# Expert loops written out, row sums on VectorE in layer 0, and halves and quarters of the probabilities added by GpSimd in layer 1

## The chip, the cores and the metric

The kernel runs on one core of one Trainium2 chip. The metric is the device time of one execution in microseconds (us), and lower is better. TensorE (PE in the rows; PEld is its weight load) multiplies matrices and transposes, VectorE (DVE), ScalarE (ACT) and GpSimd (POOL) do the rest, and SyncE (SP) issues most of the DMAs. Every engine works through a queue of its own in order; between engines only semaphores order the work.

## The reference

Two transformer layers on x of 16 batches x 256 tokens x 128 channels, all in float32. Each layer is a modulated layer norm, an attention with a gated residual, another modulated norm, and a mixture of experts with a gated residual. Cut to what matters:

```
# layer 0: causal attention, 16 heads of 8 channels, with relative keys and values
att = softmax(mask(q k^T / sqrt(8) + q . rk[t - s]))
y   = att v + sum_s att[t, s] rv[t - s];  out = y Wproj + bproj
# layer 1: sparse attention: per batch the k = 76 most important of 256 keys
importance = relu(x wi1^T + bi1) wi2^T + bi2;  top 76 keys kept
att = softmax(q k^T / sqrt(8)) over the kept keys;  out = (att v) wo^T + bo
# experts (both layers): 8 experts, the best 2 for each of 4096 tokens
layer 0: out = sum_k w_k * (gelu(x c_fc[e]) c_proj[e]);        128 -> 512 -> 128
layer 1: r = x + (gelu(x Wi[e]) * sigmoid(x Wg[e])) Wo[e];  layer norm of r, weighted
```

## The kernel before

The program is a row of blocks, each ended by a barrier of all engines: setup; for each layer norm, projections, attention, norm with the routers' logits, routing, experts, combine; and the output. `wait_ge(semaphore, n)` holds the engine's queue until the count is reached, and the instructions behind it wait too.

**Layer 0 attention** (`rel_attention_phase`, lines 510 to 765). A batch is worked through in four steps j = 0 to 3 of 64 queries; step j has 64(j + 1) keys. A global counter m counts the steps. In round m TensorE computes the scores of step m (L606, L614) into `ps_s`, four PSUM banks that hold one step only, so the scores of step m + 1 wait until VectorE is through with step m (`wait(pe, subbed, m)`). VectorE's `shift(m)` adds the causal mask (L704), takes the row maximum (L707) and subtracts it (L710); ScalarE takes the exponential (L741). Behind the scores TensorE transposes the probabilities of step m - 1 (`turn`, L629, copied back by ScalarE, L749), multiplies those of m - 2 with the relative values (`rel_values`, L642; `mask`, L716, on VectorE), and in certain steps the values of the batch (`values`, L656), a second product with a matrix of ones, `ones_diag`, that gives the row sums spread to the layout of the result (L660), the `fold` of the relative part (L669) and the output projection (`project`, L676). VectorE's `normalize` takes the reciprocal of the 128x256 sums (L721) and multiplies (L723). GpSimd prepares the masked queries (`diag`, L403; `rel`, L411) and `v_diag`, and adds the result to x (L581).

**Layer 1 attention** (`sparse_attention_phase`, lines 940 to 1172). A batch has two rounds of 128 queries, m = 2b and m = 2b + 1. GpSimd's `choose(b)` (L1148) builds the 0/1 matrix `select` of the kept keys; TensorE's `gather(b)` (L986, L989) multiplies it with the keys and values; VectorE's `spread(b)` (L1058) and ScalarE's `split_values(b)` (L1106) lay them out. TensorE's queue in an even round m = 2b is: `scores(m)` (L999), `gather(b + 1)`, `turn(m - 1, (0, 1))` (L1010), `project(b - 2)` (L1032), `turn(m - 1, (2, 3))`. In an odd round it is `scores(m)`, two turns with `values(b - 1)` (L1020) between and behind them, and `denominators(b - 1)` (L1027). `gather(b + 1)` waits for `selected`, which `choose(b + 1)` raises. VectorE's queue in a round is `normalize` (L1084, L1086; even rounds), `shift(m)` (maximum L1065, subtraction L1068), `row_sums(m - 1)` (L1074, over all 16 x 76 probabilities of a row), in even rounds `invert(b - 1)` (L1080) and `spread(b + 1)`. ScalarE copies the four transposed groups (L1119), with `gate` (L1125) between the second and the third in even rounds, and then takes the exponential `exp(m)` (L1112). GpSimd's queue sets the order at its end:

```
choose(0); memset v_diag; choose(1)
for b in range(B + 2):
    if b >= 1 and b + 1 < B: choose(b + 1)
    if 1 <= b <= B: widen(b - 1)      # waits for invert(b - 1)
    if b >= 2: add(b - 2)
```

`widen` (L1155) spreads the reciprocals of the row sums, and `denominators` transposes them.

**Experts** (`expert_phase`, lines 1432 to 1728). 39 tiles of 256 token slots. Per tile GpSimd issues two indirect DMAs that fetch token rows (L1696) and two that scatter the result (L1704), SP loads the expert's weights, and TensorE does the first layer (L1526), a transpose of a later tile's rows (L1536) and the second layer (L1545). The tiles 0 to 3 and 32 to 38 are written out; the 28 between run in hardware loops of 7 passes over four tiles (`tiles`, `Fori`). VectorE copies the indices of each tile into `token_now` (L1586, L1618) and `dest_now` (L1612), at a place that is the same in every pass of the loop, and the indirect DMAs read them there.

## Time and profile before

| what | us |
|---|---|
| median of 3 runs | 1541.46 (1540.43 to 1545.56) |
| the profiled execution, its device time | 1546.82 |
| its span in the profile | 1544.9 |
| layer 0 attention in it | 77 to 581 |
| layer 0 experts | 667 to 877 |
| layer 1 attention | 990 to 1164 |
| layer 1 experts | 1247 to 1506 |
| TensorE matmul, VectorE, ScalarE, GpSimd busy | 1246.8, 890.5, 650.9, 562.8 |

The profiled execution took 5.4 us more than the median, 0.35%. Busy time is that of the whole span; the stages have different limits, so each is read by itself. A matmul in float32 stands in the profile as two records, and the ends of matmuls are modelled, so the distance between the starts of two blocks tells more than their durations.

### The profile page before, as it was taken

The page shows a single profiled execution, that of the slowest core. Times are in us where ns is not written, and L with a number is a line of the kernel's source. Part 1 is how long each engine was busy: PE and PEld are TensorE (multiplying, and loading weights), DVE is VectorE, ACT ScalarE, POOL GpSimd, SP SyncE. Part 2 cuts the span into 40 slices and gives each one's busy share as a digit, 9 for nine tenths or more (in the row PEclk, how much of TensorE's full clock was granted, in tenths as well). Part 3 has the DMA queues.
Part 4 walks back from the last instruction along what each step waited for, and adds up shares of the span by engine and source line. Part 5 has one row for each costly group of instructions (what it writes and reads, how often), then busy time and mean ns, then how long its engine had stood idle before and what let it go on. Part 6 is the DMA issues. An engine that isn't in the chain of part 4 may idle for free. (4 is left out here: it accounts for less than half of the span.)

```text
span 1544.9 us, 46711 instructions
## 1 busy us (share of the span) xinstructions
PE 1246.8 (81%) x19038; PEld 1035.9 (67%) x19038; DVE 890.5 (58%) x2078; ACT 650.9 (42%) x1298; POOL 562.8 (36%) x636
## 2 busy tenths in 40 slices
PE   5778899988999887578877559688887569999973
PEld 4457677766777777567777444355556569999973
DVE  6455565645657644821111175899994737677664
ACT  3233343333434435024343262266765036666533
POOL 2231231211312200457777400112110437888760
PEclk7889999999999995579999858799997569999985
DMA  5632223122230002045455430000003045655536
GB/s 153 156 101 38 33 31 52 38 31 30 32 49 12 4 3 69 1 121 163 149 152 151 96 89 1 1 1 1 1 1 86 12 107 178 182 172 178 173 74 165
DMA packets 110896, 119.27 MB, mean 77 GB/s; under 512 B 28064, under 2 KB 78464, under 8 KB 110208
## 3 DMA queue, kind: packets, MB, share of 16 engines
q1 hardware_dynamic: 100736, 96.23, 24.5%
q0 software_dynamic: 9984, 20.47, 5.4%
q8 instruction: 139, 2.28, 0.6%
q14 instruction: 37, 0.30, 0.1%
HBM read 97.79 MB, written 21.91 MB: 77 GB/s over the span
## 5 line engine op out<-in xcount | busy, mean ns | idle before, releaser
L1572 ACT ACTIVATE act_x_m<-ps_h_x_m,fc_bias_x_m 128x256 f32<-128x256 f32 x468 | 196.2, 470 | 182.3 <-PE ps_h_x_m L1526 167.4
L1526 PE MATMUL ps_h_x_m<-x_T_x_m,fc_x_m 128*128 128x256 f32 x936 | 245.3, 413 | 3.0 <-issue 1.9
L1526 PEld LDWEIGHTS ps_h_x_m<-x_T_x_m,fc_x_m 128*128 128x128 f32 x936 | 227.7, 329 | 6.4 <-issue 4.3
L749 ACT ACTIVATE probT<-ps_t 128x512 f32<-128x512 f32 (+1 forms) x192 | 104.0, 591 | 194.1 <-PE ps_t L629 194.1
L1704 POOL DMA_INDIRECT y_dram<-y_x_m,dest_now_x_m x156 | 155.4, 996 | 63.2 <-issue 43.3
L1696 POOL DMA_INDIRECT x_rows_x_m<-h_dram,token_now_x_m x156 | 154.9, 993 | 52.8 <-issue 44.7
L1545 PE MATMUL ps_o_x_m<-proj_x_m,act_x_m 128*128 128x128 f32 x1248 | 154.2, 277 | 2.6 <-DVE act_x_m L1596 2.6
L1545 PEld LDWEIGHTS ps_o_x_m<-proj_x_m,act_x_m 128*128 128x128 f32 x1248 | 147.6, 194 | 3.0 <-DVE act_x_m L1596 2.8
L704 DVE TENSOR_TENSOR ps_s<-ps_s,future 128x512 f32<-128x512 f32 x64 | 44.7, 699 | 169.4 <-PE ps_s L614 169.4
L1612 DVE COPY dest_now_x_m<-dest_m 128x2 int32 (+1 forms) x78 | 14.4, 184 | 204.8 <-PE ps_o_x_m L1545 171.0
L741 ACT ACTIVATE prob<-prob 128x512 f32<-128x512 f32 (+1 forms) x64 | 81.2, 1269 | 100.9 <-DVE prob L710 100.9
L629 PE MATMUL ps_t<-ident,prob 128*128 128x128 f32 (+1 forms) x768 | 107.1, 283 | 8.5 <-ACT probT L749 7.8
L614 PE MATMUL ps_s<-e_rel,q_rel 64*32 64x64 f32 (+3 forms) x4096 | 98.8, 312 | 10.8 <-issue 10.5
L629 PEld LDWEIGHTS ps_t<-ident,prob 128*128 128x128 f32 (+1 forms) x768 | 80.6, 132 | 35.3 <-ACT probT L749 15.9
L707 DVE TENSOR_REDUCE neg_max<-ps_s 128x8 f32<-128x512 f32 (+1 forms) x64 | 95.4, 1491 | 2.2
L710 DVE TENSOR_TENSOR prob<-ps_s,neg_max 128x512 f32<-128x512 f32 (+1 forms) x64 | 95.4, 1491 | 2.2
L574 POOL COPY v_diag<-v 128x128 f32<-128x128 f32 x32 | 8.4, 291 | 231.9 <-PE ps_y L669 231.8
L1119 ACT ACTIVATE probT<-ps_t 76x512 f32<-76x512 f32 x128 | 69.0, 590 | 49.6 <-PE ps_t L1010 49.6
L614 PEld LDWEIGHTS ps_s<-e_rel,q_rel 64*32 64x32 f32 x4096 | 65.5, 109 | 36.0 <-issue 26.8
L656 PE MATMUL ps_y<-probT,v_diag 128*32 128x128 f32 x1536 | 82.4, 274 | 6.9 <-ACT upd L756 3.6
L1313 POOL TENSOR_SCALAR column_hit_m<-column_m,part_f_m,choice_id_m 128x78 f32<-128x78 f32 x64 | 48.4, 760 | 104.7 <-DVEq L1393 102.1
L1580 ACT ACTIVATE x_T_x_m<-ps_x_x_m 128x256 f32<-128x256 f32 x78 | 29.9, 384 | 129.2 <-PE ps_x_x_m L1536 129.2
(261 smaller groups left out, 2359.6 us busy)
## 6 DMA issues: line engine op xcount, KB each, us to landing
q_spread<-q_dram SPq DMA_DIRECT2D x256, 64.0 KB
fc_x_m<-L_ffn_c_fc SPq DMA_DIRECT2D x39, 256.0 KB
proj_x_m<-L_ffn_c_proj SPq DMA_DIRECT2D x39, 256.0 KB
fc_x_m<-L_ffn_Wi SPq DMA_DIRECT2D x39, 256.0 KB
fc_x_m<-L_ffn_Wg SPq DMA_DIRECT2D x39, 256.0 KB
proj_x_m<-L_ffn_Wo SPq DMA_DIRECT2D x39, 256.0 KB
got_c_m<-y_dram SPq DMA_DIRECT2D x32, 256.0 KB, 5.2
h_dram<-h_rows_m SPq DMA_DIRECT2D x16, 256.0 KB, 2.3
```

The source lines that it names most:

```text
L614: x = pe.matmul(ps_s[rows(i), 2 * z + hp, s * n:(s + 1) * n], a.q_rel[64 * z:64 * (z + 1), b % 2, tile, hp, :], a.e_rel[64 * z:64 * (z + 1 ...
L629: x = pe.transpose(ps_t[0:ks, t % 2, p * P:(p + 1) * P], prob[:, m % 2, p, at:at + ks], k.ident[:, :])
L656: pe.matmul(ps_y[rows(p), 0, P * half:P * (half + 1)], v_diag[:, b % 2, ch, 4 * p + h, :], view(probT[:, half + ch, p, 0, :], TB * h, [[QU ...
L707: dve.tensor_reduce(neg_max[:, m % 2, :, :], split(ps_s[:, 0, :], m), AX.X, ALU.max, negate=True).then_inc(maxed, 1)
L710: dve.tensor_tensor(split(prob[:, m % 2, 0, :], m), split(ps_s[:, 0, :], m), view(neg_max[:, m % 2, :, :], 0, [[2, GROUPS], [1, 2], [0, n] ...
L741: act.activation(p_, p_, ACT.Exp).then_inc(expd, 1)
L749: act.activation(probT[0:ks, store(m, ch), :, (2 * j + s) % 4, :], ps_t[0:ks, t % 2, :].rearrange("p (g c) -> p g c", g=GROUPS), ACT.Copy) ...
L1526: m = pe.matmul(ps_h[:, l, g, f % 2, :], fc[:, slot, l, f:FF:FK], x_T[:, slot % 2, :], start=True, stop=True)
L1545: m = pe.matmul(ps_o[:, s % 2, h * P:(h + 1) * P], act1[:, s % 2, f, h * P:(h + 1) * P], proj[:, s, f, :], start=f == 0, stop=f == FK - 1)
L1572: m = act.activation(out[:, slot % 2, f, :], ps_h[:, l, g, f % 2, :], ACT.Tanh if l else ACT.Gelu, scale=0.5 if l else 1.0, bias=fc_bias[: ...
L1696: pool.indirect_dma_start(out=x_rows[:, slot, h, :], out_offset=None, in_=k.h_dram, in_offset=bass.IndirectOffsetOnAxis(ap=token_now[:, sl ...
L1704: pool.indirect_dma_start(out=k.y_dram, out_offset=bass.IndirectOffsetOnAxis(ap=dest_now[:, slot, h:h + 1], axis=0), in_=y[:, slot, h, :], ...
```

## The change

It has three parts.

1. **Experts.** The hardware loops go; all 39 tiles are written out with constants as semaphore counts, and the indirect DMAs read their indices straight from `r.token` and `r.dest`. The copies into `token_now` and `dest_now` and their semaphore go.
2. **Layer 0 attention.** The products with `ones_diag` go. VectorE sums the rows of each step (`row_sums`), inverts the 32 sums of a row once a batch (`invert`), GpSimd lays the reciprocals on a diagonal (`spread_inv`), four matmuls bring them to the result's layout (`denominators`), and `normalize` copies and multiplies. The orders on TensorE, GpSimd and ScalarE change, and two small tables replace `ones_diag`.
3. **Layer 1 attention.** GpSimd adds the two halves of each row of 76 probabilities and then the halves of that (`fold_rows`), VectorE's `row_sums` sums the 19 that are left. `project` moves behind the second turn, `normalize` behind `shift`, its copy to ScalarE, `gate` behind the exponential.

```diff
 rel_attention_phase, GpSimd:
+            def spread_inv(b):
+                pool.wait_ge(inv_ready, b + 1)
+                wait(pool, inv_turned, b)
+                pool.tensor_tensor(inv_diag[:, :, :, :], view(row_inv[:, b % 2, 0, :], 0, [[NB, GROUPS], [1, NB], [0, BLOCK]]),
+                                   view(a.own_query[:, 0, :], 0, [[0, GROUPS], [0, NB], [1, BLOCK]]), ALU.mult).then_inc(inv_spread, 1)
-            for b in range(B + 1):
+            for b in range(B + 2):
                 if b + 1 < B:
                     wait(pool, score, NP * b)
                     diag(pool, a, b + 1)
+                if b >= 2:
+                    add(b - 2)
+                if b + 1 < B:
                     rel(pool, a, b + 1)
+                if 1 <= b <= B:
+                    spread_inv(b - 1)
+                if b + 1 < B:
                     values(b + 1)
-                if b >= 1:
-                    add(b - 1)
 TensorE:
-                        for p in range(GROUPS):
-                            pe.matmul(ps_y[rows(p), 1, P * half:P * (half + 1)], a.ones_diag[:, h, :],
-                                      view(probT[:, half + ch, p, 0, :], TB * h, [[QUADRANT, 16], [1, TB]]),
-                                      start=False, stop=False, skip_group_check=True)
+            def denominators(b):
+                pe.wait_ge(inv_spread, b + 1)
+                for p in range(GROUPS):
+                    x = pe.matmul(ps_y[rows(p), 1, :], a.head_rows[:, :, :], inv_diag[:, p, :, :],
+                                  start=False, stop=True, skip_group_check=True)
+                x.then_inc(inv_turned, 1)
...
+                if j == 0:
+                    if exists(m - 2):
+                        rel_values(m - 2)
+                    if exists(m - 1):
+                        turn(m - 1, 0)
+                        values(b - 1, 0, (2, 3))
+                        turn(m - 1, 1)
+                elif j == 1:
+                    if exists(m - 1):
+                        turn(m - 1, 0)
+                        turn(m - 1, 1)
+                    if exists(m - 2):
+                        rel_values(m - 2)
+                    if b >= 1:
+                        values(b - 1, 1, (0, 1, 2, 3))
+                elif j == 2:
+                    if exists(m - 1):
+                        turn(m - 1, 0)
+                        turn(m - 1, 1)
+                    if exists(m - 2):
+                        rel_values(m - 2)
+                    if b >= 1:
+                        denominators(b - 1)
+                        fold(b - 1)
+                else:
+                    if exists(m - 1):
+                        turn(m - 1, 0)
+                    if exists(m - 2):
+                        rel_values(m - 2)
+                    if b >= 1:
+                        project(b - 1)
+                    if exists(m - 1):
+                        turn(m - 1, 1)
+                        values(b, 0, (0, 1))
 VectorE (row_sums behind shift and mask, invert where j == 0):
+                dve.tensor_reduce(row_sum[:, b % 2, :, 2 * j:2 * j + 2], split(prob[:, m % 2, 0, :], m), AX.X, ALU.add).then_inc(summed, 1)
...
+                dve.reciprocal(row_inv[:, b % 2, :, :], row_sum[:, b % 2, :, :]).then_inc(inv_ready, 1)
...
-                dve.reciprocal(rden[:, :], ps_y[:, 1, :]).then_inc(rden_ready, 1)
+                dve.tensor_copy(inv_y[:, :], ps_y[:, 1, :]).then_inc(inv_copied, 1)

 sparse_attention_phase, TensorE:
                 if exists(m - 1):
                     turn(m - 1, (0, 1))
-                if u == 0 and b >= 2:
-                    project(b - 2)
                 if u == 1 and 1 <= b <= B:
                     values(b - 1, (0, 1))
                 if exists(m - 1):
                     turn(m - 1, (2, 3))
+                if u == 0 and b >= 2:
+                    project(b - 2)
 VectorE:
-                dve.wait_ge(expd, m + 1)
-                dve.tensor_reduce(row_sum[:, m // 2 % 2, m % 2, :], prob[:, m % 2, :, :, :].rearrange("p g h r -> p (g h) r"),
-                                  AX.X, ALU.add).then_inc(summed, 1)
+                dve.wait_ge(quartered, m + 1)
+                dve.tensor_reduce(row_sum[:, m // 2 % 2, m % 2, :], part_sum[:, m % 2, :, :], AX.X, ALU.add).then_inc(summed, 1)
...
+                if exists(m):
+                    shift(m)
                 if u == 0 and b >= 2:
                     normalize(b - 2)
-                if exists(m):
-                    shift(m)
 ScalarE:
+                if u == 0 and b >= 2:
+                    copy_inv(b - 2)
                 if exists(m - 1):
                     copy(m - 1, (0, 1))
-                if u == 0 and b >= 2:
-                    gate(b - 2)
-                if exists(m - 1):
                     copy(m - 1, (2, 3))
                 if exists(m):
                     exp(m)
+                if u == 0 and b >= 2:
+                    gate(b - 2)
 GpSimd:
+            def fold_rows(m):
+                r = prob[:, m % 2, :, :, :].rearrange("p g h r -> p (g h) r")
+                pool.wait_ge(expd, m + 1)
+                wait(pool, quartered, m)
+                pool.tensor_tensor(half_sum[:, :, :], r[:, :, 0:KEPT // 2], r[:, :, KEPT // 2:KEPT], ALU.add).then_inc(halved, 1)
+                pool.wait_ge(halved, m + 1)
+                wait(pool, summed, m - 1)
+                pool.tensor_tensor(part_sum[:, m % 2, :, :], half_sum[:, :, 0:KEPT // 4], half_sum[:, :, KEPT // 4:KEPT // 2],
+                                   ALU.add).then_inc(quartered, 1)
...
             for b in range(B + 2):
+                if 1 <= b <= B:
+                    fold_rows(2 * b - 1)
+                    widen(b - 1)
                 if b >= 1 and b + 1 < B:
                     choose(b + 1)
-                if 1 <= b <= B:
-                    widen(b - 1)
+                if b < B:
+                    fold_rows(2 * b)
                 if b >= 2:
                     add(b - 2)

 expert_phase:
-        def tiles(eng, step, first=0, last=XTILES):
-
-            for j in range(first, UNROLL):
-                step(j // UNROLL, j % UNROLL)
-            with eng.Fori(1, LOOP_END) as i:
-                for s in range(UNROLL):
-                    step(i, s)
...
-                dve.tensor_copy(token_now[:, s, :], r.token[:, bass.ds(2 * (j + UNROLL), 2)]).then_inc(token_ready, 1)
...
-                                            in_offset=bass.IndirectOffsetOnAxis(ap=token_now[:, slot, h:h + 1], axis=0)).then_inc(x_in[slot], 16)
+                                            in_offset=bass.IndirectOffsetOnAxis(ap=r.token[:, 2 * j + h:2 * j + h + 1], axis=0)).then_inc(x_in[slot], 16)
```

## Rows read from the trace of the kernel before

**Rows 1.** Windows by stage: stretch, length, busy PE PEld DVE ACT POOL, PEclk, DMA, GB/s

```profile
77.00:581.00 504.00, 439.53 (x14078) 354.53 (x14063) 294.06 (x290) 192.26 (x273) 115.76 (x79) 0.96 0.21 35
...
990.00:1164.00 174.00, 150.78 (x1468) 98.13 (x1467) 155.39 (x160) 115.08 (x193) 31.03 (x63) 0.97 0.01 1
...
1247.00:1506.00 259.00, 235.22 (x1326) 228.78 (x1326) 166.68 (x544) 143.22 (x352) 187.97 (x196) 0.95 0.54 159
```

**Rows 2.** Timeline of one batch of layer 1 attention: start, duration, engine, line

```profile
1062.52 0.79 PE L999 MATMUL ps_s<-k_diag,qT 32*128 32x304 f32 x8
...
1063.25 0.67 PE L986 MATMUL ps_g<-select,kv 128*128 128x76 f32 x4
1063.43 1.42 DVE L1065 TENSOR_REDUCE neg_max<-ps_s 128x16 f32<-128x1216 f32 x1
...
1064.88 1.43 DVE L1068 TENSOR_TENSOR prob<-ps_s,neg_max 128x1216 f32<-128x1216 f32 x1
...
1066.22 1.41 DVE L1074 TENSOR_REDUCE row_sum<-prob 128x16 f32<-128x1216 f32 x1
...
1067.66 0.35 DVE L1080 RECIPROCAL row_inv<-row_sum 128x32 f32<-128x32 f32 x1
...
1068.08 0.40 POOL L1155 COPY inv_wide<-row_inv 128x256 f32<-128x256 f32 x1 [8.34 <-DVE row_inv L1080]
...
1068.48 1.07 PE L1010 MATMUL ps_t<-ident,prob 128*76 128x128 f32 x8 [1.15 <-ACT prob L1112]
...
1069.14 0.93 POOL L1148 TENSOR_SCALAR select<-places,rank 128x76 f32<-128x76 f32 x2
...
1072.85 0.79 PE L999 MATMUL ps_s<-k_diag,qT 32*128 32x304 f32 x8
```

**Rows 3.** Timeline of the first rounds of layer 1 attention, at the lower clock

```profile
987.83 0.94 POOL L1148 TENSOR_SCALAR select<-places,rank 128x76 f32<-128x76 f32 x2 [78.56 <-SPq L941]
...
988.82 1.14 PE L986 MATMUL ps_g<-select,kv 128*128 128x76 f32 x4 [10.40 <-POOL select L1148]
...
997.20 3.24 PE L1010 MATMUL ps_t<-ident,prob 128*76 128x128 f32 x16
```

**Rows 4.** Windows around one of TensorE's gaps in layer 0 attention, columns as Rows 1

```profile
329.00:336.00 7.00, 0.23 (x4) 0.00 (x0) 0.00 (x0) 0.00 (x0) 0.00 (x0) 0.86 0.51 68
336.00:339.00 3.00, 2.98 (x35) 2.18 (x36) 1.33 (x2) 0.37 (x1) 0.00 (x0) 0.50 0.02 7
...
342.00:346.00 4.00, 3.94 (x164) 2.89 (x160) 2.43 (x3) 1.43 (x1) 0.52 (x2) 1.00 0.02 4
```

**Rows 5.** Groups by line: busy us, mean ns of one, idle before

```profile
L707 DVE TENSOR_REDUCE neg_max<-ps_s 128x8 f32<-128x512 f32 (+1 forms) x64 | 95.4, 1491 | 2.2
...
L721 DVE RECIPROCAL rden<-ps_y 128x256 f32<-128x256 f32 x16 | 28.1, 1757 | 26.7 <-PE ps_y L669 26.7
```

**Rows 6.** Timeline of one batch of layer 0 attention, VectorE and TensorE

```profile
193.30 0.70 DVE L704 TENSOR_TENSOR ps_s<-ps_s,future 128x512 f32<-128x512 f32 x1 [0.81 <-PE ps_s L614]
...
200.30 0.70 DVE L704 TENSOR_TENSOR ps_s<-ps_s,future 128x512 f32<-128x512 f32 x1 [1.31 <-PE ps_s L614]
...
207.51 0.40 PE L660 MATMUL ps_y<-probT,ones_diag 128*32 128x128 f32 x8
207.73 0.40 PE L656 MATMUL ps_y<-probT,v_diag 128*32 128x128 f32 x8
...
221.07 0.70 DVE L704 TENSOR_TENSOR ps_s<-ps_s,future 128x512 f32<-128x512 f32 x1 [0.81 <-PE ps_s L614]
```

**Rows 7.** TensorE's waits in layer 0 attention: total, times, longest us

```profile
PE ps_y L669 <- issue: 17.3, 10, 6.0
PE ps_s L614 <- issue: 10.5, 7, 6.8
```

**Rows 8.** GpSimd's timeline in the layer 0 experts, in the loop and behind it

```profile
745.76 0.96 POOL L1696 DMA_INDIRECT x_rows_x_m<-h_dram,token_now_x_m  x1 [0.30 <-issue]
...
864.10 0.97 POOL L1704 DMA_INDIRECT y_dram<-y_x_m,dest_now_x_m  x1 [0.31 <-issue]
```

More of the change, by code:

```diff
@@ L732, in _ @@
                     mask(m - 2)
+                if exists(m - 1):
+                    row_sums(m - 1)
+                if j == 0 and 1 <= b:
+                    invert(b - 1)
                 if b >= 1 and j == 2:
@@ L1428 @@
 UNROLL = 4
-LOOP_END = XTILES // UNROLL - 1
 def expert_phase(nc, k, r, name, weights, gated):
@@ L1480, in exists, with count @@
         def exists(j):
-            return not isinstance(j, int) or 0 <= j < XTILES
-        def tiles(eng, step, first=0, last=XTILES):
-            for j in range(first, UNROLL):
-                step(j // UNROLL, j % UNROLL)
-            with eng.Fori(1, LOOP_END) as i:
-                for s in range(UNROLL):
-                    step(i, s)
-            for j in range(UNROLL * LOOP_END, last):
-                step(j // UNROLL, j % UNROLL)
-        def ring(i, s, n):
-            return (s + n) % UNROLL, i + (s + n) // UNROLL + 1
+            return 0 <= j < XTILES
+        def count(j):
+            return j // UNROLL + 1
         @block.sync
@@ L1547, in second_layer @@
                 m.then_inc(out_ready, 1)
-            def step(i, s):
-                j = UNROLL * i + s
+            for j in range(-2, XTILES):
                 if exists(j + 1):
-                    first_layer(i, s)
+                    first_layer(j + 1)
                 if exists(j + 2):
-                    turn(i, s)
+                    turn(j + 2)
                 if exists(j):
-                    second_layer(j, s)
-            tiles(pe, step, first=-2)
+                    second_layer(j)
         @block.scalar
         def _(act):
-            def step(i, s):
-                n = UNROLL * i + s + 1
+            for n in range(-1, XTILES + 1):
                 if exists(n):
-                    slot, _ = ring(i, s, 1)
+                    slot = n % UNROLL
                     for g in range(2):
@@ L1660, in normalize @@
                 m.then_inc(y_ready, 1)
-            def step(i, s):
-                j = UNROLL * i + s
+            for j in range(-1, XTILES):
                 if gated:
@@ L1722, in step @@
                     pool.nop(nofuse=True)
-                    gather(j + UNROLL, s)
-            tiles(pool, step, last=XTILES + 1)
+                    gather(j + UNROLL)
             for s in range(UNROLL):
```

192 lines of the change are left out of this document (92 added, 100 removed).

## The prediction

> **What bounds the kernel now.** I read the table of windows by stage first [rows 1]. Each stage ends in a barrier, so each is costed alone. Layer 0 attention takes 504 us, and TensorE works for 440 of them, at nearly the full clock (0.96). Layer 1 attention takes 174 us, with VectorE busy for 155 and TensorE for 151. The layer 1 experts keep TensorE busy for 235 of 259 us and GpSimd for 188.
>
> Then the timelines. A batch of layer 1 attention lasts 1072.85 - 1062.52 = 10.33 us [rows 2]. TensorE has one pause in it, 1.15 us at 1068.48, while it waits for ScalarE's exponential; VectorE has half a microsecond. So both engines are nearly full, and the ring that sets the pace is: scores, gather, turn, ScalarE's copies and exponential, the next round's turns and values, scores. What the reader should see as well is who stands where on GpSimd. `select` for the next gather is made at 1069.14 by L1148. TensorE wants it in the next even round, right behind the scores of 1072.85. It is done 2.8 us early, and the profile shows no wait for it in the steady state. Only at the start, where `select` is late, does it show one: L986 begins 0.05 us after L1148 has ended [rows 3].
>
> In layer 0 attention a batch without a long stall takes 221.07 - 193.30 = 27.8 us [rows 6]. The stage's mean is 504 / 16 = 31.5. The rest is start and end, and stalls of TensorE for which the profile names no releaser ("issue"): 27.8 us on two lines [rows 7], some 36 with the small ones, one of them 6.8 us long [rows 4, 7].
>
> **Layer 1 attention: what the new order on GpSimd does.** This decides the forecast. Before, `choose(b + 1)` was the first thing in GpSimd's iteration b. Now `fold_rows(2b - 1)` and `widen(b - 1)` stand ahead of it. `widen(b - 1)` waits for `invert(b - 1)`, and on VectorE that stands behind `shift(2b)`, thus behind the scores of round 2b. But TensorE wants `choose(b + 1)` directly behind these scores, for `gather(b + 1)`. Queued behind that gather are the turns of round 2b - 1, and behind them ScalarE's copies and exponential: the whole ring. It is no deadlock, since nothing in the chain needs the gather, but TensorE stands still for all of it.
>
> The chain from the start of the scores (1062.52) to the new start of the gather, from rows 2: maximum begins after 0.91; subtraction 1.45 later (1064.88 - 1063.43); its end 1.34 later (1066.22 - 1064.88); the multiplication of `normalize`, now here, 0.45 (of its kind of size 256; its row isn't shown, bounds 0.35 to 0.7 by the neighbours); the row sum of 304 instead of 1216 numbers, a quarter of 1.41 plus a fixed part, 0.43 (bounds 0.35 and 1.41); from reciprocal to `widen` 0.42; `widen` 0.40; `select` 0.93; TensorE 0.05 later [rows 3]. Sum 6.4 us. Before, the gather began 0.73 us after the scores (1063.25). So each gather is 5.7 us late. The quarter sums don't add to this: the exponential of the odd round has ended before, and GpSimd's two additions of 608 and 304 numbers, at its 0.72 us for 256 in `add` and 1.9 for 1024 in `diag` (estimates 1.3 and 0.8), are done within the 3.7 us that the subtraction takes to end.
>
> What is saved: VectorE's 2 x 1.0 us of summing and a copy of 0.4, all in time that is now idle; and `project` and `gate` out of the way of the third and fourth turn, about 0.2 us on the ring. New period 10.33 + 5.7 - 0.2 = 15.8. The stall meets the gathers of b = 1 to 14, since `choose(0)` and `choose(1)` come ahead of the loop: 14 x 5.5 = **+77 us**.
>
> **The clock.** TensorE would now stand idle for 5.7 of 16 us. After its gap of 6.8 us in layer 0 the granted clock is 0.50 for the next 3 us and 1.00 again after 6 [rows 4]; all three gaps of 4.5 to 6.8 us in that stage are followed by 3 to 6 us at 1.2 GHz (the other clocked windows lie after the start and after one gap of 1.3 us; gaps of 2 us had none). At the lower level the gather takes about 0.94 us more (1.14 against 0.67 for each half) [rows 2, 3] and eight transposes 1.62 instead of 1.07 (3.24 / 2) [rows 2, 3], two lots: 2.0 us a batch in all on the ring. I take it for 85% of the batches, 1.7: 14 x 1.7 = **+24 us**. The bounds are 0 (no fall) and a clock that stays low through the odd round too, whose 4.4 us from turn to scores would become 8.8: +4.4 more, +90 us in all.
>
> The Trainium skill says, in TensorE: Matmul & The Clock Gate, Part 1: The HAM clock gate, that the low clock is the state at rest, that idling brings it on, and that sustained work lifts it. By that rule every batch would pay the 2.0, giving 28 us instead of 24. The trace agrees with it in all three gaps.
>
> **Layer 0 attention.** TensorE loses 12 blocks of four products with ones per batch, at 0.22 us each (207.73 - 207.51), 2.64 us [rows 6], and gains one block of double width, 0.43: -2.2 a batch. VectorE gains row sums as long as L707's maxima, 95.4 / 16 = 5.96 us a batch, and 0.35 for the small reciprocal, and swaps 1.76 for a copy of 0.42 [rows 5]: +5.0 on 294 / 16 = 18.4 [rows 1], of 27.8. It becomes nearly as full as TensorE. Most of the sums lie where it waits for scores. In step j = 3 they don't: mask, maximum and subtraction take 0.70 + 2 x 2.29 and the gaps, 5.35; behind it stand the mask product 0.45 and the sum over step 2, 1.8, together 7.65, where the next scores were ready after 7.00 (200.30 - 193.30) [rows 6]. So this step gets 0.65 longer and the next 0.2; step 1, where TensorE led, gets 1.2 shorter, and the last about 0.1. Sum -0.5 a batch, **-7 us**. Between -2.2 x 16 = -35 (TensorE sets all) and +14 (only the two late sums count) I stay with the step by step value. `spread_inv` on GpSimd, 1024 numbers like `diag` at 1.9 us, ends some 5 us before TensorE wants it; were it late, it would be a stall like the one above, at 16 times the lateness.
>
> The stalls at "issue" fall while 16 DMAs of the next batch's queries run, and hit the engine that goes through most instructions. It has 11% fewer now (192 of some 1,760 records a batch). I take **-10 us** of the 36 and their slow clock, bounds 0 and -36. The tail of the last batch loses 8 x 0.22 less 0.43 of products and 1.3 us of reciprocal, **-3**. The added tables, some 23 small GpSimd instructions, lie in the first norm, where GpSimd idles for 17 us behind its tables, so they cost nothing; without that cover, 6 us.
>
> **Experts.** Removing loops pays where the loop costs. An indirect DMA starts 0.30 us after its predecessor's end in the loop and 0.31 in the written-out part behind it [rows 8]. Four of these at 1.29 us fill a tile of the layer 0 experts, 5.15 us, in both parts, and the layer 1 tiles are filled by TensorE (235 of 259 us) [rows 1]. The removed copies are VectorE's, which is half idle; only the first ones, ahead of the first gather, count. **-1 us** for both layers, bounds -3 and +10 (a new stall at "issue" in either).
>
> The Trainium skill, Runtime: NRT & Kernel Launch, Instruction fetch mechanics, says that a taken branch out of the fetched window waits for a fetch. By it the passes would pay, and their going would gain. The trace disagrees: no gap stands at a pass's end.
>
> **Sum.** -7 - 10 - 3 + 77 + 24 - 1 = +80 us on the profiled 1546.8, thus 1627; that execution is 5.4 above the median of 1541.46, so against the median **1621.5 us**.
>
> **Rivals.**
> 1. The clock holds at 2.4 GHz: 1621.5 - 24 = 1598. For it: the work behind the gap is dense. Against it: rows 4. Chance 0.17.
> 2. The clock stays low through the odd rounds: +66 more, 1688. For it: in the first rounds it stayed at 0.5 for 11 us, though TensorE was busy for most of them. Chance 0.1.
> 3. The late gather doesn't bind, because GpSimd gets to `choose(b + 1)` before TensorE wants it. Then the stage gains 3 us, and the kernel takes 1541.5 - 24 = 1517. This is the case on the other side. It decides if `invert(b - 1)` ends before the scores of round 2b; the queue on VectorE speaks against it. Chance 0.05.
> 4. Layer 0 gains nothing, since VectorE's sums delay every step: 1642. For it: VectorE comes to 23.4 of 27.3 us. Chance 0.12.
> 5. Layer 0 gains its -35 and most of the stalls: 1580. Chance 0.08.
> 6. The loops did cost: 14 ends of a pass at the mean stall of 36 / 27 = 1.3 us give -18, 1603. Chance 0.02.
>
> My forecast has 0.46. The range 1575 to 1670 leaves out rivals 2 and 3 and the edges of the others, under 0.2 together. Faster and slower are counted from 0.3%, 4.6 us, about what a measurement of this kernel tells from no change: faster 0.05, same 0.01, slower 0.94.
>
> **What would show it.** In the profile after: TensorE's waits should have a line `ps_g` <- POOL `select` of about 14 x 5.7 = 80 us; the distance of even rounds' scores should be near 17.5 us; the granted clock in the stage should lie between 0.7 and 0.9; the stage should last 270 to 280 us. VectorE's row sums there should take about 0.4 us, and in layer 0 a clean batch about 27.3. If the wait on `select` is missing, the reasoning on the queue is wrong, and with it the sign. If the stage is right and the total isn't, look at layer 0, where the stalls of TensorE are the least certain term.

## The result, and the profile after

The changed kernel takes 1645.74 us (median of 4, 1639.13 to 1649.74) against 1540.95 for the kernel before on the same chip (4 runs, 1534.19 to 1545.56). The ratio is 1.068, 95% interval 1.063 to 1.073: 105 us slower. The forecast was 1621.5 in a range of 1575 to 1670. The ratios here and below are of the executions within 1.5% of the fastest of their kernel, so they can differ a little from the quotient of the medians.

The profiled execution took 1639.13 us (span 1637.1), the lowest of its four, while the one of before was above its median. The two spans differ by 92.2 us, the medians by 104.8; the stages below are read from the spans. First the windows by stage of the changed kernel, columns as in [rows 1]: layer 0 attention, layer 0 experts, layer 1 attention, layer 1 experts.

```profile
77.00:579.00 502.00, 417.12 (x12624) 331.92 (x12624) 364.71 (x369) 192.77 (x273) 144.96 (x92) 0.91 0.22 35
...
664.00:874.00 210.00, 166.20 (x1014) 156.01 (x1014) 16.56 (x39) 79.62 (x196) 152.99 (x156) 0.96 0.53 148
...
984.00:1262.00 278.00, 184.51 (x1473) 122.52 (x1474) 122.19 (x144) 123.20 (x210) 100.27 (x130) 0.79 0.00 1
...
1344.00:1600.00 256.00, 231.55 (x1326) 226.77 (x1326) 159.77 (x472) 143.00 (x352) 185.56 (x196) 0.96 0.54 162
```

Two stages stand out against [rows 1]. Layer 1 attention went from 174 to 278 us, and its granted clock from 0.97 to 0.79. Layer 0 attention kept its length although TensorE has 22 us less work in it, VectorE has 71 more, and the clock fell from 0.96 to 0.91.

Cut exactly (first `select` or first masked addition to the end of the last `add`), the 92 us are: layer 1 attention 175.9 to 277.9, **+102.0**; layer 0 attention 501.4 to 501.3, **-0.1**; ahead of it -1.3; between the two attentions -2.8; behind the second -5.6.

TensorE's largest waits of the changed kernel (total us, times, longest):

```profile
PE ps_g L1046 <- POOL select L1211: 87.1, 15, 10.4
...
PE ps_s L628 <- DVE prob L753: 40.3, 23, 4.1
```

The first is new. Its longest, 10.4, is the start of the stage, as in [rows 3]; the other 14 are 5.47 us each. The second was 10.4 us before. The timeline of one batch of layer 1 attention, as [rows 2]:

```profile
1056.03 1.13 PE L1046 MATMUL ps_g<-select,kv 128*128 128x76 f32 x4 [5.47 <-POOL select L1211]
...
1057.81 3.23 PE L1070 MATMUL ps_t<-ident,prob 128*76 128x128 f32 x16
...
1062.83 1.07 PE L1070 MATMUL ps_t<-ident,prob 128*76 128x128 f32 x8 [0.63 <-ACT prob L1170]
...
1067.19 0.80 PE L1059 MATMUL ps_s<-k_diag,qT 32*128 32x304 f32 x8
...
1068.06 1.42 DVE L1125 TENSOR_REDUCE neg_max<-ps_s 128x16 f32<-128x1216 f32 x1 [2.51 <-PE ps_s L1059]
...
1069.52 1.42 DVE L1129 TENSOR_TENSOR prob<-ps_s,neg_max 128x1216 f32<-128x1216 f32 x1
1070.86 0.41 DVE L1144 TENSOR_TENSOR y_T<-ps_y,inv_y 128x256 f32<-128x256 f32 x1
1071.19 0.46 DVE L1135 TENSOR_REDUCE row_sum<-part_sum 128x16 f32<-128x304 f32 x1
1071.68 0.35 DVE L1140 RECIPROCAL row_inv<-row_sum 128x32 f32<-128x32 f32 x1
1072.10 0.40 POOL L1229 COPY inv_wide<-row_inv 128x256 f32<-128x256 f32 x1 [2.17 <-DVE row_inv L1140]
1072.47 0.93 POOL L1211 TENSOR_SCALAR select<-places,rank 128x76 f32<-128x76 f32 x2
...
1073.46 1.14 PE L1046 MATMUL ps_g<-select,kv 128*128 128x76 f32 x4 [5.47 <-POOL select L1211]
```

Read it from 1067.19, the scores of the even round. Everything between them and the gather at 1073.46 is a chain: maximum, subtraction, `normalize`, row sum, reciprocal on VectorE, then `widen` and only then `select` on GpSimd. It takes 6.27 us. In [rows 2] `select` came 1 us after `widen` too, but the gather that it served was a period later. The period is now 1073.46 - 1056.03 = 17.43 us (17.2 to 17.9 over the stage), was 10.33. Behind the gap the sixteen transposes take 3.23 us instead of 2.1: the lower of the two clocks, 1.2 GHz. In the odd round eight transposes take 1.07 us again (1062.83), which is the full clock.

### The profile page after: what moved, and what is told of

It is laid out like the page before. It is cut to its first block and busy times, and to the rows that moved or that the text cites. A ratio compares the mean times of both kernels' runs of the same rounds, so it can differ in the third digit from the quotient of the medians.

```text
span 1637.1 us, 42882 instructions
## 1 busy us (share of the span) xinstructions
PE 1252.8 (77%) x17630; PEld 1035.5 (63%) x17630; DVE 912.8 (56%) x1991; ACT 659.6 (40%) x1314; POOL 662.7 (40%) x739
## 5 line engine op out<-in xcount | busy, mean ns | idle before, releaser
L1744 POOL DMA_INDIRECT y_dram<-y_x_m,dest_m x156 | 154.8, 992 | 62.6 <-issue 42.3
L1735 POOL DMA_INDIRECT x_rows_x_m<-h_dram,token_m x156 | 153.0, 981 | 50.3 <-issue 42.0
L1673 DVE TENSOR_TENSOR y_x_m<-ps_o_x_m,out_rows_m 128x256 f32<-128x256 f32 x39 | 16.6, 425 | 188.0 <-PE ps_o_x_m L1606 188.0
L650 PE MATMUL ps_t<-ident,prob 128*128 128x128 f32 (+1 forms) x768 | 113.0, 295 | 0.0
L650 PEld LDWEIGHTS ps_t<-ident,prob 128*128 128x128 f32 (+1 forms) x768 | 89.9, 141 | 23.3 <-issue 21.2
L628 PE MATMUL ps_s<-kT,q_diag 32*128 32x256 f32 (+3 forms) x1024 | 59.7, 345 | 54.3 <-DVE prob L753 40.3
L1125 DVE TENSOR_REDUCE neg_max<-ps_s 128x16 f32<-128x1216 f32 x32 | 45.6, 1424 | 93.5 <-PE ps_s L1059 93.5
L1220 POOL TENSOR_TENSOR half_sum<-prob 128x608 f32<-128x608 f32 x32 | 40.6, 1267 | 138.6 <-ACT prob L1170 138.6
L765 DVE TENSOR_REDUCE row_sum<-prob 128x8 f32<-128x512 f32 (+1 forms) x64 | 94.4, 1475 | 0.0
L1070 PE MATMUL ps_t<-ident,prob 128*76 128x128 f32 x512 | 85.9, 323 | 9.9 <-ACT prob L1170 8.7
```

What stands on the lines that cost most here:

```text
L650: x = pe.transpose(ps_t[0:ks, t % 2, p * P:(p + 1) * P], prob[:, m % 2, p, at:at + ks], k.ident[:, :])
L765: dve.tensor_reduce(row_sum[:, b % 2, :, 2 * j:2 * j + 2], split(prob[:, m % 2, 0, :], m), AX.X, ALU.add).then_inc(summed, 1)
L1070: x = pe.transpose(ps_t[0:KEPT, t % 2, h * P:(h + 1) * P], prob[:, m % 2, p, h, :], k.ident[:, :])
L1735: pool.indirect_dma_start(out=x_rows[:, slot, h, :], out_offset=None, in_=k.h_dram, in_offset=bass.IndirectOffsetOnAxis(ap=r.token[:, 2 * ...
L1744: pool.indirect_dma_start(out=k.y_dram, out_offset=bass.IndirectOffsetOnAxis(ap=r.dest[:, 2 * j + h:2 * j + h + 1], axis=0), in_=y[:, slot ...
```

## The experiments

Each kernel ran against the kernel before on the same chip. Ratios are those; times of different sessions aren't compared, since the kernel before had medians of 1546.7, 1544.3, 1654.8 and 1550.7 us in the four. What the third session has more lies outside the attentions: in a profile of it (the short sums below) layer 1 attention takes 177.4 us, as in E1, but the stretch between the attentions 449.5 instead of 402 and the one behind the second 423.9 instead of 376. So the lengths of the attention stages are read across sessions. With the changed code, layer 0's took 501.3, 500.1, 500.1 and 495.4 us in four profiles (changed kernel, E1, the layer 0 part alone, the filled gap of layer 1), so a difference of under 6 us says little. "E1" names the first kernel below, on which most others build.

**Is it the order on GpSimd?** E1, the changed kernel with the two calls as they were ordered before:

```diff
-                if 1 <= b <= B:
-                    fold_rows(2 * b - 1)
-                    widen(b - 1)
                 if b >= 1 and b + 1 < B:
                     choose(b + 1)
+                if 1 <= b <= B:
+                    fold_rows(2 * b - 1)
+                    widen(b - 1)
```

> The changed kernel with select for the next gather back ahead of fold_rows and widen on GpSimd; everything else as changed. My theory (the late select holds TensorE in 14 of 16 batches of layer 1, and the low clock behind it costs more): the attention stage of layer 1 falls from 277 us to 172 to 176, its granted clock rises from 0.79 to 0.97, the line ps_g <- select vanishes from TensorE's waits, and the kernel takes 1535 to 1545 us. Rival (the quarter sums on GpSimd and the extra wait ahead of the subtraction carry a good part): the stage keeps more than 190 us and the kernel stays above 1560.

Measured: 1535.2 us, ratio 0.992 (0.990 to 0.994). The stage and TensorE's wait in it:

```profile
979.90:1157.20 177.30, 158.14 (x1472) 100.24 (x1472) 119.90 (x144) 120.47 (x209) 100.60 (x129) 0.95 0.01 1
```
```profile
PE ps_g L1046 <- POOL select L1211: 10.4, 1, 10.4
```

Fourteen of the fifteen waits are gone, and 100.6 of the 102 us with them. The stage is a little longer than expected (172 to 176). What is left of the quarter sums is a stage of 177.3 against 175.9, with a period of 10.28 us: they gain nothing.

**The order alone, in the kernel before**, without quarter sums:

```diff
-                if b >= 1 and b + 1 < B:
-                    choose(b + 1)
                 if 1 <= b <= B:
                     widen(b - 1)
+                if b >= 1 and b + 1 < B:
+                    choose(b + 1)
```

> The kernel before, with only the two calls on GpSimd swapped: widen for the last batch ahead of choose for the next. No quarter sums, nothing else of the change. If the order on GpSimd alone is the cause, this kernel shows the whole loss: the chain from scores to gather is longer than in the changed kernel, since VectorE's row sum over 1216 numbers (1.41 us against 0.47) is in it, so about 6.2 us a batch and 1.7 for the clock, 14 x 7.9 = 110 us, 1650 in all. Rival (the calls of the quarter sums are what makes select late): under 1570.

Measured: 1667.6 us, ratio 1.078 (1.075 to 1.081), 121 us; the stage takes 294.7.

```profile
1099.87 1.14 PE L986 MATMUL ps_g<-select,kv 128*128 128x76 f32 x4 [6.12 <-POOL select L1148]
...
1119.16 1.14 PE L986 MATMUL ps_g<-select,kv 128*128 128x76 f32 x4 [6.12 <-POOL select L1148]
```

Two swapped calls cost more than the whole change does: their chain holds a sum over 1216 numbers (1.41 us against 0.46). So in the changed kernel the quarter sums make the loss smaller, since VectorE's sum has come to lie on the chain. The expectation of 110 us was 11 short. The wait was forecast well (6.2 us, measured 6.12), but the period grew by more than the wait and the 1.7 us put down for the clock: it alternates between 18.3 and 19.3 us, in the mean 8.5 more than before instead of 7.9.

**How much of it is the clock?** The changed kernel, with the gap of TensorE filled:

```diff
+                if u == 0 and 1 <= b and b + 1 < B:
+                    for i in range(40):
+                        pe.transpose(ps_g[:, 3 * P:4 * P], k.ident[:, :], k.ident[:, :])
                 if u == 0 and b + 1 < B:
                     gather(b + 1)
```

> The changed kernel with 40 transposes of the identity into an unused part of ps_g ahead of each gather of layer 1 from the third batch on; they add work whose result is used nowhere, about 5.4 us at full clock, and fill the 5.47 us in which TensorE waits for select. If the clock behind the stall is what makes the period 17.4 instead of 15.8, it falls by about 1.6 us, the stage from 277 to about 254, the kernel by 24 us to about 1620, with the granted clock there near 1. Rival (the 1.6 us is not the clock but the chain itself): the period stays at 17.4 or grows, the kernel takes 1645 or more.

Measured: 1612.3 us, ratio 1.043 (1.039 to 1.046), where 1620 was expected. The stage is 254.2 us long, its granted clock 0.97.

```profile
1063.77 0.67 PE L1046 MATMUL ps_g<-select,kv 128*128 128x76 f32 x4 [0.95 <-POOL select L1214]
...
1074.06 4.59 PE L1101 MATMUL ps_g<-ident 128*128 128x128 f32 x40
...
1079.59 0.67 PE L1046 MATMUL ps_g<-select,kv 128*128 128x76 f32 x4 [0.95 <-POOL select L1214]
```

The gather takes 0.67 instead of 1.14 us and the period is 15.82. Useless work on the waiting engine takes 277.9 - 254.2 = 23.7 us off the stage. So of the 102 us about 78 are the late `select` and 24 the clock behind it.

**Layer 0: one part alone.** The kernel before with the layer 0 part of the change only (`rel_tables`, `rel_attention_phase` and its tiles replaced by those of the change), and the kernel before with only the experts written out:

```diff
-from before: rel_tables, rel_attention_phase, layer0_attention
+from after:  rel_tables, rel_attention_phase, layer0_attention
```

> The kernel before with the layer 0 part of the change alone (row sums, the inverse spread and turned, the new order of values). My prediction gave it -20 us (1521); the profile of the changed kernel shows its stage at 500.6 us, as before, so it should be 1536 to 1544. The kernel with layer 0 as before stood at 525 us for the same stage, with the same code of that stage as before; so a third view is that the code behind decides: then the value here says nothing of the changed kernel.

Measured: 1537.7 us, ratio 0.999 (0.995 to 1.004); stage 500.1 us. The layer 0 part alone does nothing that can be measured.

```diff
-from before: expert_phase (loops over passes of tiles)
+from after:  expert_phase (written out)
```

> The kernel before with only the experts written out. My prediction gave -1 us. From the last add of layer 1's attention to the end all kernels with written-out experts took 376 us and those with loops 382, so I expect -6 to -8 us in the stages behind layer 0. What I want to see is layer 0's attention, whose code is untouched: if it takes 525 us here too (as in the kernel with layer 0 as before), the written-out experts slow a stage that runs ahead of them, and the kernel stands near 1560; if it takes 500, the whole is near 1533.

Measured: 1532.4 us, ratio 0.993 (0.988 to 0.998). From the end of layer 0's attention to the end it needs 957.8 us against 964.0, of which 5.8 in the layer 1 experts (first gather to last scatter 256.6 to 250.8): TensorE waits there for gathered rows 10.5 us (2 times) instead of 14.0 (6 times), its busy time for the same 1326 records is 231.2 us instead of 235.2, and VectorE has 469 instructions instead of 542. The stretch behind layer 1's attention took 375.6 to 378.1 us in the seven profiles with written-out experts outside the third session, and 380.0 to 381.8 in the four with loops, so the gain holds. The trace of the kernel before also shows pauses of VectorE in the layer 1 experts that the changed kernel and this one don't have:

```profile
DVE act_x_m L1596 <- issue: 9.5, 28, 0.7
...
1365.35 0.69 DVE L1596 SCALAR_TENSOR_TENSOR act_x_m<-act_x_m 128x512 f32<-128x512 f32 x1 [0.68 <-issue]
```

There is one in each of the 28 tiles of the loop and none in the tiles written out. 22 last 0.24 us, and six 0.7 us, at every fourth tile (1317.6, 1341.4, 1365.3, 1389.2, 1413.3, 1438.5): there a pass of the loop ends. GpSimd has one pause of 1.7 us, at 1431.7. That these pauses make the gathers late for TensorE is likely, but not shown.

The profiled execution took 1550.3 us, 18 more than the median (the 12 lie between 1527 and 1555), and has a layer 0 stage of 512 us, which is neither of the two values expected. The kernel before took 1530 to 1562 us on this chip, but for one outlier.

**E1 with layer 0 as before**, run in two sessions:

```diff
-from after:  rel_tables, rel_attention_phase, layer0_attention
+from before: rel_tables, rel_attention_phase, layer0_attention
```

> As the kernel with select put back first, but with layer 0's attention and its tables as in the kernel before. Read beside that one it gives the worth of the layer 0 part. If it is worth nothing (its stage took 500.6 us in both profiles), the two differ by less than 3 us; by my prediction the layer 0 part was worth 20 us, and this kernel would be 20 slower. Beside the kernel before it shows the joined experts and the quarter sums without the late select: 1533 to 1541.

> The same code as the kernel with layer 0 as before, once more. There it took 1562 us (1557 to 1569), its stage of layer 0 526 us against 501 in the kernel before with the same code of that stage, most of the difference in stalls of TensorE without a releaser. With the experts alone written out the stage took 512 and the times fell into two lots, around 1528 and around 1552. If the slowness belongs to this kernel's code, it is back: 1555 to 1570. If it belonged to that session, it is 1528 to 1545, and the layer 0 part is worth nothing as in the two profiles.

Measured: ratio 1.010 (1.007 to 1.014) in the first session, 0.992 (0.987 to 0.997) in the second. E1 had 0.992 on the chip of the first session: there the layer 0 part looks worth 27 us (1562.2 against 1535.2), more than the 20 forecast, and by the second ratio nothing, as with loops behind it. The stage took 526 and 513 us, with the code of a stage that took 501 in the kernel before. TensorE's waits of the first of the two:

```profile
PE ps_s L614 <- issue: 13.2, 7, 7.4
PE ps_s L606 <- issue: 11.0, 4, 4.2
PE ps_y L669 <- issue: 11.0, 9, 5.0
PE ps_y L660 <- issue: 10.0, 4, 7.0
```

Against [rows 7], L606 and L660 are new (0.8 and 1.5 us before). With this code of the stage, the stalls without a releaser stand at the same places in the kernels with looped experts (near 158, 336 and 376 us), and at others in all three with written-out ones: 3.4 to 5.1 us between 179 and 187 us, 6.2 to 7.0 between 220 and 228, 3.3 to 4.2 between 257 and 265. So code that runs much later goes with where they fall.

The changed code of the stage shows the same. Its stalls of over 2.5 us stand near 238, 280, 362 and 402 us in the changed kernel, in E1 and in the short sums below, and near 147, 187, 341 and 460 both with the loops of before behind the stage (the layer 0 part alone) and in the kernel with the filled gap of layer 1, which differs from the changed one only by 560 transposes, all of them behind this stage. So it isn't the loops as such.

The places are settled by that, the length isn't. With the code of before the stage took 499 to 503 us with loops behind it and 512 to 526 with written-out experts; but the three profiled executions of the latter lay 18, 7 and 8 us above the medians of their kernels, and with the changed code the two sets of places gave 500 and 501 against 495 and 500 us. The second session's ratio is also lower than the first's by more than both intervals.

**Does moving the code move the stalls?** The kernel before with empty instructions ahead of the stage:

```diff
+            for _ in range(600):
+                pe.nop(nofuse=True)
             for m in range(PAIRS + 4):
```

> The kernel before with 600 empty instructions on TensorE's queue ahead of layer 0's attention; nothing else differs. They compute nothing and only move the code of the stage. In two kernels with looped experts the stage's stalls without a releaser stood at the same places (158, 217, 336, 376, 537 us) and the stage took 501 and 503 us; in three with written-out experts and the same code of the stage they stood at others (150, 185, 227, 262, 400, 440, 480) and it took 512, 526 and 513. If the place of the code in memory decides, the stalls move here too, to the same lines in neighbouring batches or to other lines, and the stage, counted from its first masked addition, comes out anywhere from 495 to 526. If the stalls hang on the work itself (its DMAs, its lines), they stay where they were and the stage takes 501 to 503. The whole kernel is slower by what the 600 instructions take ahead of the stage beyond the 5.9 us in which TensorE waits there, 5 to 30 us by my guess.

Measured: ratio 0.999 (0.994 to 1.004), stage 498.6 us. The stalls stayed: 6.8 us ending at 333.6 (336.0 before), 5.2 at 373.1 (6.0 at 376.1), 4.2 at 158.9 (4.5 at 158.7). This speaks against the place in TensorE's code. But the page counts 46711 instructions in both and the instruction queue moved 2.29 MB against 2.28, so the profile doesn't show that the code grew by all 600, and the 5 to 30 us that they were expected to cost aren't there either. Inconclusive.

**What does TensorE wait for in these stalls?** The traces have the single DMA packets, and they answer a part of it. The largest stall of the changed kernel lasts from 395.4 to 403.3 us; the two fences are the DMA queues from 395.4 to 399.9 and from 399.9 to 402 us:

```profile
q1 hardware_dynamic: 355, 0.32, 57.1%
```
```profile
q1 hardware_dynamic: 21, 0.01, 6.1%
q8 instruction: 1, 0.02, 5.1%
```

q1 carries the query loads of the next batch, q8 blocks of 16384 bytes of instructions. For 4.7 us no block comes. As the loads run out, one starts, at 400.1; it ends at 401.9, and TensorE goes on 1.5 us later. It is so everywhere: between the first and the last masked addition of this stage, the 14 profiles have 145 waits of over 1 us without a releaser, and each of them ends 1.2 to 1.8 us after the end of a q8 packet. Of TensorE's instructions in three of the profiles 13% start at such a distance, so this is hardly chance. TensorE waits there for its own instructions, 26 to 40 us a stage.

Why the block is late is less sure. All 63 stalls of over 2.5 us overlap the traffic of the query loads. The q8 packet that ends them starts 5.8 to 12.6 us after the one before, where the median in the stage is 4.0 to 4.2, and in 35 of them it starts less than 0.5 us before the loads' traffic ends. That the blocks queue behind the loads fits this; no run took the loads away.

**Why does the layer 0 part gain nothing?** The timeline of the changed kernel, from step 3 of one batch to step 0 of the next, TensorE alone:

```profile
448.46 0.64 PE L677 MATMUL ps_y<-probT,v_diag 128*32 128x128 f32 x16
451.02 0.67 PE L628 MATMUL ps_s<-kT,q_diag 32*128 32x64 f32 x16 [1.92 <-DVE prob L753]
451.63 0.86 PE L636 MATMUL ps_s<-e_rel,q_rel 64*32 64x64 f32 x64
452.41 1.81 PE L663 MATMUL ps_r<-probT,ev 128*32 128x64 f32 x64
454.16 1.97 PE L650 MATMUL ps_t<-ident,prob 128*128 128x128 f32 x8
```

In step 3 TensorE has fewer products than before and is done 1.92 us ahead of VectorE's subtraction. The scores behind that wait take what they take at the full clock (0.67 and 0.86 us), but the products behind them run at 1.2 GHz: 1.81 us for 64 of them, where 1.10 is usual, and 1.97 for eight transposes instead of 1.09 (the granted clock from 452.6 to 456.0 is 0.50). VectorE's step from 0 to 1 takes over 6.3 us in 12 of the 16 batches and 5.2 to 5.6 in the other four, although the wait is there in some of these too. Three kernels test the links, all on E1.

VectorE's row sums cut to the first 8 keys of a row, so most of the summing is left out and the denominators are other numbers:

```diff
-split(prob[:, m % 2, 0, :], m)
+split(prob[:, m % 2, 0, :], m)[:, :, :, 0:TB]
```

> The kernel with select first, but VectorE's row sums in layer 0 take only the first 8 keys of each row, so the denominators are wrong sums and most of the summing is left out (about 1.1 us of the mean 1.47 of each of 64). If VectorE's sums are what delays the scores' subtraction in step 3, the wait <- DVE prob falls from 40 us to about the 10 of the kernel before, and the stage of layer 0 from 500 to 465 to 480. Rival (the subtraction is late because of the mask, maximum and subtraction chain of 5.35 us against less work of TensorE in that step, whatever the sums cost): the wait stays at 30 us or more and the stage gains under 8 us.

Measured: stage 494.9 us, ratio 0.987 (0.982 to 0.993), which for the stage is within the scatter of the same code without the cut (495.4 to 501.3). The sums and the wait:

```profile
L765 DVE TENSOR_REDUCE row_sum<-prob x64: 206/207/220, 87.2 to 561.3; 128x8 f32<-128x64 f32 x64
```
```profile
PE ps_s L628 <- DVE prob L753: 39.4, 22, 4.1
```

The sums fell from 94.3 to 13 us and the wait from 40.3 to 39.4. VectorE's load isn't what TensorE waits for; it is the chain mask, maximum, subtraction, whose 5.35 us no longer have enough work of TensorE beside them.

Filling the wait with useless work:

```diff
                         values(b, 0, (0, 1))
+                        pe.wait_ge(copied, turns(m) - 1)
+                        for i in range(12):
+                            pe.transpose(ps_t[:, turns(m) % 2, 0:P], k.ident[:, :], k.ident[:, :])
```

> The kernel with select first, and in step 3 of layer 0 twelve transposes of the identity more, ahead of the next scores, into the half of ps_t that is overwritten next; their result is used nowhere. They fill the 1.9 us in which TensorE waits for VectorE's subtraction. If the low clock behind that wait is what keeps the time from step 0 to step 1 at 6.6 us instead of 5.3, the stage of layer 0 gets 12 to 20 us shorter and its granted clock rises from 0.91 to above 0.95. Rival (the step is set by VectorE, the clock costs nothing): no change or up to 5 us longer.

Measured: ratio 0.985 (0.979 to 0.992), stage 480.0 us, 20 less than E1's.

```profile
283.36 1.53 PE L742 MATMUL ps_t<-ident 128*128 128x128 f32 x12
285.32 0.67 PE L628 MATMUL ps_s<-kT,q_diag 32*128 32x64 f32 x16 [0.43 <-DVE prob L756]
285.92 0.86 PE L636 MATMUL ps_s<-e_rel,q_rel 64*32 64x64 f32 x64
286.71 1.10 PE L663 MATMUL ps_r<-probT,ev 128*32 128x64 f32 x64
287.74 1.09 PE L650 MATMUL ps_t<-ident,prob 128*128 128x128 f32 x8
```

The scores start no earlier, but what stands behind them runs at full clock. Between 79 and 557 us the granted clock is 0.97, in E1 0.92, and the step from 0 to 1 has a median of 5.15 us, in E1 6.58.

Putting real work there instead, the values of all four heads in step 3 as before:

```diff
-                        values(b - 1, 0, (2, 3))
...
-                        values(b, 0, (0, 1))
+                        values(b, 0, (0, 1, 2, 3))
```

> The kernel with select first, and in layer 0 the values of the first half taken for all four heads in step 3, as in the kernel before, none in step 0. TensorE then has about 0.9 us more in step 3, where it waits for VectorE, and as much less in step 0. If the placement of that work is what took the gain, the wait <- DVE prob falls by half and the stage gets 8 to 15 us shorter; if VectorE's row sums set every step, nothing changes (within 3 us).

Measured: ratio 0.990 (0.985 to 0.995), stage 485.9 us. The wait stayed at 34.6 us in all, so the gain isn't the one expected. The step from 0 to 1 holds 0.65 us less work (not 0.9, as I had put it). The single wait of a batch fell only from 1.92 to some 1.48 us, and fewer steps pay at the lower clock: five of the 16 take 5.0 us and ten 5.9 to 8.4, with 6.18 in the median and a granted clock of 0.94. Which of the two makes how much of the 14 us wasn't separated.

Both together, with eight transposes:

> The kernel with select first, with the values of all four heads of the first half in step 3 and eight transposes of the identity more behind them, whose result is used nowhere. The values in step 3 took 14 us off the stage of layer 0 (500 to 486), twelve transposes alone 20. If both act on the same wait and clock, the two together give 478 to 484 us for the stage and the kernel about 1518; if they add up, 466 to 472 and about 1506.

Measured: ratio 0.977 (0.973 to 0.982), stage 475.9 us, between the two expectations, so neither holds as it was put. This kernel beats both the kernel before and the changed one: the written-out experts, the row sums, `select` first, and TensorE kept busy through the wait of step 3.

## Why the prediction was right, and where it wasn't

**Layer 1 attention, +77 and +24: right, by its own steps.** Predicted were a wait on `select` of about 80 us, a period of 17.5, a stage of 270 to 280 us, a clock of 0.7 to 0.9 and +101; measured 87.1 with the old 10.4 of the start in it, 17.43, 277.9, 0.79 and +102.0. The experiments split it at 78 and 24, where the sum had 77 and 24, with a period of 15.82 without the clock against 15.8 forecast. The chain from scores to gather was estimated at 6.4 us and is 6.27; `normalize` 0.41 and the row sum 0.46 were estimated at 0.45 and 0.43. The two additions on GpSimd take 1.27 and 0.83 us, estimated 1.3 and 0.8. Of the rivals, the first (the clock holds) and the third (the gather doesn't bind) fell; the second is excluded by the odd round's transposes, 1.07 us for eight at 1062.83. The saving of 0.2 us a batch on the ring was not there (10.28 against 10.33, in E1).

The Trainium skill, TensorE: Matmul & The Clock Gate, Part 1: The HAM clock gate, has the low clock as the state after idling and activity as what lifts it. The trace agrees: filling the gap with useless products raised the granted clock from 0.79 to 0.97 in layer 1's attention and from 0.92 to 0.97 in layer 0's.

**Layer 0 attention, -20: wrong, it is 0.** This is the failed step, and rival 4's outcome came by another mechanism than its own. Its three terms:
- Steady steps, -7. VectorE's 64 steps give medians from step 0 to 1, 1 to 2, 2 to 3, 3 to 0 of 5.29, 7.61, 8.73, 7.00 before and 6.61, 6.66, 7.78, 7.26 after. Step 1 got 0.95 shorter (1.2 forecast), the last one 0.95 (0.1), step 3 0.26 longer (0.65). But the step behind it, forecast at +0.2, is +1.3: that is the clock, which the prediction counted in layer 1 only. It had read that gaps of 2 us are followed by no fall, and had passed over the one of 1.3 us that was; here one of 1.92 us is followed by it in most batches. Together -0.3 a batch, 450.9 - 445.7 = -5 us. That this is near the -7 is luck, as the two largest misses nearly cancel: the last step gained 0.85 us more than forecast, and the step behind step 3 took 1.1 more.
- Stalls at "issue", -10. What the steps took beyond these medians is 478.4 - 450.9 = 27.5 us before and 481.1 - 445.7 = 35.4 after, **+8**. The waits without a releaser alone sum to 36.3 us before and 40.0 after (37.4 to 40.9 in the other three profiles with this code), with a tenth fewer instructions on TensorE. So the reasoning from their number doesn't hold. The rest of the +8 is steps slowed otherwise, and wasn't taken apart. This term is 18 of the 20 us that are missing.
- Tail, -3: 22.9 us from the last masked addition to the end before, 20.2 after. Right.

Filling the wait returned 20 us. That this equals the gain forecast is a coincidence: it lies in the step from 0 to 1 (1.43 us a batch less in the median than E1's), where the forecast had no gain at all. It shows that the steady steps could have given some 27 us (medians summed to 423.5 instead of 450.9), four times the -7, without the lower clock.

**Experts, -1: mis-sized**, outside its bounds of -3 and +10. Alone they are worth 0.7% (0.2 to 1.2%), 6 us of it in view, nearly all in the layer 1 experts, where the prediction counted only the copies ahead of the first gather. The prediction's "no gap stands at a pass's end" was read from GpSimd's rows in layer 0 and is wrong for layer 1: VectorE pauses 0.7 us at six ends of a pass there, and 0.24 us in each other tile of the loop. So the loops did cost, as the sixth rival had it, though a third of its 18 us. That TensorE waits less often for gathered rows is seen; whether the pauses or the copies made it wait wasn't tried.

**The sum.** 1645.7 is 24 above 1621.5: +20 for layer 0 attention, +1 for layer 1's, -9 for the experts and the short stretches around them (measured -9.7, forecast -1), and 12 because the prediction carried the 5.4 us by which its execution lay above the median, while the one profiled after lies 6.6 below its own. The experts' gain hides a part of what layer 0 lost.

## What to carry to other kernels

On an engine's in-order queue, ask of each instruction put ahead of another whose result it waits for, and whether that chain begins at the reader of the one behind it: two swapped calls cost 121 us here while neither got slower. Taking work off the busiest engine pays only in steps where it isn't already early; where it becomes early, it waits, and then pays again at the lower clock. Products without use in such a wait are a quick test for that, and here also the remedy.

## What was unexpected of the hardware

- A wait of TensorE of 1.92 us, once a batch, is followed in most batches by 1.2 GHz for some 3.8 us (1.81 and 1.97 us for work of 1.10 and 1.09). At 1.48 us it still is in about two thirds of them; shortened to 0.43 us by filler, it mostly isn't. The length of the wait alone doesn't decide: in the kernel before, waits of 2.86 us (at 96.7) and 2.14 us (at 123.5) were followed by a granted clock of 1.00.
- The stalls of TensorE without a releaser, up to 8.4 us long, end 1.2 to 1.8 us after a packet of the instruction queue, all 145 of over 1 us in 14 profiles. They move when only code behind the stage differs. At three of the largest (ending at 336.0 us in the kernel before, 225.3 with the experts alone, 403.3 in the changed kernel) the loads' traffic ends 0.2 us behind the stall's end, 2.9 us and 3.0 us ahead of it, so it isn't the end of the traffic itself that frees TensorE. The Trainium skill, Runtime: NRT & Kernel Launch, Instruction fetch mechanics, has an engine fetch its instructions by a DMA queue of its own, in blocks, a cost mostly hidden. The trace agrees on the queue and the blocks; the cost isn't hidden here, 26 to 40 us of a stage of 500.
